# A power on GpSimd between neighbouring indirect transfers, and a new fixed order of all engines' steps

## What is computed

```python
x = _layernorm(x + attn0(x))   # causal, 16 heads of 8, no bias
x = _layernorm(x + ffn0(x))    # top 2 of 8 experts
x = _layernorm(x + attn1(x))   # full, 16 heads of 8, biases
x = _layernorm(x + ffn1(x))    # top 3 of 15 experts, and a shared one

# ffn0, hidden 256
gates, expert_idx = jax.lax.top_k(softmax(xf @ gate_w + gate_b), 2)
h = relu(einsum('nc,ech->neh', xf, w1) + b1)
expert_out = einsum('neh,ehc->nec', h, w2) + b2
out = einsum('ne,nec->nc', weights, expert_out)

# ffn1, hidden 128, the shared expert 256
topk_w, topk_idx = jax.lax.top_k(softmax(xt @ gate_w.T), 3)
topk_w = topk_w / (sum(topk_w) + 1e-20)
h = einsum('td,efd->etf', xt, fc1_w) + fc1_b
a = gelu(h[..., F:]) * h[..., :F] * geglu_mult
yexp = einsum('etf,edf->etd', a, fc2_w) + fc2_b
y = einsum('etd,te->td', yexp, comb) + shared(xt)
```

## Time and profile before

| | |
|---|---|
| median of 3 runs | 944.91 us (943.97 to 946.92) |
| the profiled execution, its span | 1048.6 us |
| instructions | 23098 |
| TensorE busy | 808.7 us, 77% |
| VectorE busy | 657.8 us, 63% |
| ScalarE busy | 500.0 us, 48% |
| GpSimd busy | 429.6 us, 41% |

### The profile page before, as it was taken

How to read it: one execution, slowest core, us unless ns; L and a number is a source line. 1 busy time by engine, 2 the same in 40 slices (tenths; PEclk the granted TensorE clock), 3 DMA queues, 4 the chain that set the end, 5 groups by cost and what they waited for, 6 DMA issues and landing times.

```text
span 1048.6 us, 23098 instructions
## 1 busy us (share of the span) xinstructions
PE 808.7 (77%) x7666; PEld 537.5 (51%) x7666; DVE 657.8 (63%) x1916; ACT 500.0 (48%) x971; POOL 429.6 (41%) x654
## 2 busy tenths in 40 slices
PE   4789878779896878779888797777877795877750
PEld 3456555546664655446545453443444684756640
DVE  2867757666543776767478676786744442565674
ACT  2255545555463565636766465674544252223310
POOL 3002332322144455642354544635366304555565
PEclk9678989989998899888989987987757898899885
DMA  5875866776647551673655543323030387766533
GB/s 122 182 203 149 180 166 178 174 206 157 160 124 147 115 122 44 137 207 109 154 132 122 134 110 75 93 52 72 23 105 33 119 258 242 208 180 188 160 88 83
DMA packets 118772, 144.51 MB, mean 138 GB/s; under 512 B 13155, under 2 KB 92673, under 8 KB 118657
## 3 DMA queue, kind: packets, MB, share of 16 engines
q1 hardware_dynamic: 106689, 121.27, 45.9%
q0 software_dynamic: 10240, 20.99, 7.2%
q10 hardware_dynamic: 1728, 0.79, 0.3%
HBM read 89.78 MB, written 54.41 MB: 138 GB/s over the span
## 4 chain that ended last, share of the span: by engine, by line
PE 26%; DVE 13%; issue 11%; another core or an unknown queue 8%; ACT 4%; DMA 4%; POOL 3%; ACTq 1%; SPq 0%; POOLq 0%; DVEq 0%
DVE mp L1383 4%; PE bank_O L1207 3%; PE bank_FH L1289 3%; PE bank_N L1301 3%; PE pair_T L1188 3%; DMA G<-yd,ypos 2%; ACT P L1021 2%; PE pair_S L1166 2%; PE pair_T L1301 2%; POOL xs L945 1%; DVE X L1588 1%; POOL G L959 1%; PE bank_O L1289 1%; PE bank_M L1127 1%
## 5 line engine op out<-in xcount | busy, mean ns | idle before, releaser
L1383 DVE TENSOR_REDUCE mp<-pair_S 128x4 f32<-128x1024 f32 (+1 forms) x248 | 270.7, 1092 | 149.4 <-PE pair_S L1166 106.0
L1021 ACT ACTIVATE P<-pair_T 128x768 f32<-128x768 f32 (+1 forms) x256 | 234.6, 916 | 122.7 <-PE pair_T L1188 82.6
L959 POOL DMA_INDIRECT G<-yd,ypos x160 | 154.7, 967 | 144.5 <-DMA yd<-yb 57.2
L945 POOL DMA_INDIRECT xs<-X,ypos x160 | 159.6, 997 | 91.9 <-DVE ypos L1535 44.4
L1207 PE MATMUL bank_O<-P,V 128*18 128x256 f32 (+1 forms) x2048 | 131.4, 402 | 2.8 <-issue 2.3
L1188 PE MATMUL pair_T<-QK 51*128 51x256 bf16 (+1 forms) x1024 | 105.9, 282 | 35.3 <-ACT P L1021 27.3
L1166 PE MATMUL pair_S<-QK 48*128 48x256 bf16 (+1 forms) x992 | 101.4, 282 | 20.8 <-DVE mp L1383 12.4
L904 POOL TENSOR_TENSOR rstd<-mv,half 128x2 f32<-128x2 f32 x48 | 9.7, 201 | 213.6 <-DVE mv L1432 211.9
L1207 PEld LDWEIGHTS bank_O<-P,V 128*18 128x18 f32 x2048 | 59.2, 107 | 55.9 <-issue 31.4
L1188 PEld LDWEIGHTS pair_T<-QK 51*128 51x128 bf16 x1024 | 49.1, 100 | 66.7 <-ACT P L1021 38.3
L1150 PE MATMUL pair_T<-bmat 64*128 64x128 bf16 (+1 forms) x544 | 50.9, 265 | 25.2 <-ACT P L1021 20.2
(11 more groups left out here) (172 smaller groups left out, 1437.2 us busy)
## 6 DMA issues: line engine op xcount, KB each, us to landing
QK<-wtab SPq DMA_DIRECT2D x62, 257.0 KB
W<-w_in SPq DMA_DIRECT2D x46, 321.0 KB
yd<-yb SPq DMA_DIRECT2D x53, 256.0 KB
stk<-parts SPq DMA_DIRECT2D x32, 384.0 KB
QK<-stk SPq DMA_DIRECT2D x64, 192.0 KB
xs<-zeros SPq DMA_DIRECT2D x19, 512.0 KB, 5.7
xp<-xs SPq DMA_DIRECT2D x33, 256.0 KB
QK<-stk SPq DMA_DIRECT2D x64, 128.0 KB
```

What stands on the lines that cost most here:

```text
L945: pool.indirect_dma_start(xs[g % 2][0:reach(a) * PAGE], bass.IndirectOffsetOnAxis(ypos[L][:, 2 * b + blk, k:k + 1], 0), X[:, 2 * b + blk, ...
L959: pool.indirect_dma_start(G[i][:, blk, k, :], None, yd[g][0:reach(q) * PAGE], bass.IndirectOffsetOnAxis(ypos[L][:, 2 * b + blk, k:k + 1], 0))\
L1021: act.activation(P[:, i:i + 2, 0:n], pair["T"][:, :].rearrange("p (h c) -> p h c", h=2)[:, :, 0:n], ACT.Exp, scale=SCALE)\
L1383: dve.tensor_reduce(mp[:, a % 2, 0:n, :, 0, p].rearrange("p a r -> p r a"), S, AX.X, ALU.max, negate=True)\
```

## The change

Two things are changed. The list `PLAN` is no longer made by `lay_out`'s play through, but by sorting the steps by a fixed table `BEGINS`, one number for each step. And behind every scatter, and every gather of layer 0, that is followed on POOL directly by another scatter or layer-0 gather, POOL runs a pause: a power of 128x2 values from `half` into the tile `idle`, which nobody reads. That makes 142 pauses, 106 behind scatters and 36 behind layer-0 gathers. A pause waits by a semaphore for the pause before it. No other instruction waits for a pause. The gathers of layer 1 have none. The steps themselves and what they wait for are the same.

```diff
+BEGINS = {
+    "load_xT": (0, 42, 1327, 1896, 2903, 6929, 8462, 10050, 11599, 13183, 14789, 16392, 17960, 19492, 21142, 26465,),
...
 def lay_out(steps):
...
-    while len(order) < len(steps):
-        best = None
...
-        order.append((at, key))
...
-    return [(key[0], key[1:]) for _, key in order]
+    begins = {}
+    for name, times in BEGINS.items():
+        begins.update(zip(sorted(key for key in steps if key[0] == name), times))
+    order = sorted(steps, key=begins.get)
...
+    return [(key[0], key[1:]) for key in order]
...
+POOL_STEPS = ("residual_bias", "inverse_std", "route_diff", "route_pos_mul", "scatter", "gather")
+ON_POOL = [(name, x) for name, x in PLAN if name in POOL_STEPS]
+PAUSES = [step for step, after in zip(ON_POOL, ON_POOL[1:])
+          if all(name == "scatter" or name == "gather" and x[0] < NB for name, x in (step, after))]
...
+        idle = sb("idle", [D, 2])
...
+            def pause(step):
+                if step in PAUSES:
+                    i = PAUSES.index(step)
+                    if i:
+                        pool.wait_ge(paused.sem, i)
+                    pool.tensor_tensor(idle[:, :], half[:, 1, :], half[:, 0, :], ALU.pow).then_inc(paused.sem, 1)
...
+                pause(("scatter", (a, blk, k)))
...
+                pause(("gather", (q, blk, k)))
```

More of the change, by code:

```diff
@@ L411, in plan @@
     return lay_out(steps)
-ENGINES = ("PE", "DVE", "ACT", "POOL", "SP")
-TILING = {"scores": 1, "scores_T": 1, "weigh_V": 2}
-SWITCH = 0.1
-def lay_out(steps):
[L421 to L441, removed]
-    while len(order) < len(steps):
-        best = None
[L444 to L459, removed]
-        order.append((at, key))
[L461 to L474, removed]
-    return [(key[0], key[1:]) for _, key in order]
@@ L478 @@
+def lay_out(steps):
+    begins = {}
+    for name, times in BEGINS.items():
+        begins.update(zip(sorted(key for key in steps if key[0] == name), times))
+    order = sorted(steps, key=begins.get)
+    place = {key: i for i, key in enumerate(order)}
+    assert all(place[k] < place[key] for key, step in steps.items() for k in step[4] if k in place)
+    return [(key[0], key[1:]) for key in order]
 PLAN = plan()
+POOL_STEPS = ("residual_bias", "inverse_std", "route_diff", "route_pos_mul", "scatter", "gather")
@@ L704, in build @@
         out_stored = signal("out_stored")
+        paused = signal("paused")
         def last_norm(k, q):
```

121 lines of the change are left out of this document (added), and 111 rows, old and new, of the table BEGINS.

## The result

The changed kernel takes 997.06 us (median of 4 runs, 986.85 to 998.29) where the kernel before takes 945.91 us (943.97 to 947.50) on the same chip. The ratio is 1.050, 95% interval 1.044 to 1.056: slower by 51 us. The prediction was 937.0 us and a range up to 960.

The account below looks back on a forecast made before the run. No single engine was taken as full; POOL matters only where its transfers stand on the chain. +7.9 + 3.05 − 4.9 − 15 = −8.9 us on 1048.6, scaled to 944.91, gave 937.0 us, range 916 to 960.

Parts of the forecast that it names:

- the new order: All 3897 steps: most stay near their place, only three places differ in a priced way, −4.9 and −15 us.
- The pauses on the chain: 13 neighbouring transfers before 819 us, +7.9 us, and five pauses in batch 31's scatters, +3.05 us; sum +11.0.
- all other pauses I cost at nothing: Pauses off the chain on POOL: covered by POOL's wait for DVE; without that cover up to 76 us.
- The price of a pause: Between two transfers on POOL: starts 1.88 us apart instead of 1.26, costing 0.61 us more; upper bound 1.13 us.
- the slower rival: Pauses on the chain cost 1.13 us each and later combines give nothing: +13 us, about 957 us; chance 0.29.
- The loads of x: Batch 8's xT load is issued up to 6.8 us earlier, shortening TensorE's wait near 135 us: −4.9 us.
- Layer 1's page stretch: Shared_fc rows and norm powers move behind pages or gathers, and TensorE waits less for hT: −15 us.
- 140 or less: Sign in the after profile: this many us from layer 1's first gather to the last end means the page case holds.
- the page case: Rival: layer 1's page stretch gives most of its 38 us, −27 us in all, about 920 us; chance 0.10.
- no gain from pauses: Spacing transfers removes no disturbance, as DVE's combine beside them mostly runs at its minimum; the sum stays +11.0 us.
- Powers that slow VectorE: Rival: pauses stretch DVE instructions beside them, +7.7 us on the chain, about 944 us in all; chance 0.04.
- The clock: Rival: TensorE's granted clock shifts with the order, 0.02 of 0.90 being 18 us either way; chance 0.04.

Follow-up runs that it names:

- e14: The changed kernel without its pauses (new order alone), on a chip where the kernel before takes 944.33 us: 980.37 us, ratio 1.037.
- e2: The changed kernel without its pauses (new order alone), on a chip where the kernel before takes 1064.45 us: 1097.69 us, ratio 1.025.
- e6: The changed kernel without its pauses (new order alone), on a chip where the kernel before takes 1064.53 us: 1103.69 us, ratio 1.039.
- e9: The changed kernel without its pauses (new order alone), on a chip where the kernel before takes 1058.12 us: 1088.30 us, ratio 1.033.
- e18: The changed kernel, unaltered, on another chip where the kernel before takes 947.79 us: 986.44 us, ratio 1.040.
- e5: The changed kernel, unaltered, on a chip where the kernel before takes 1064.53 us: 1040.26 us, ratio 0.978.
- e13: The kernel before, unaltered, profiled again on a chip where its other runs take 944.33 us: 948.69 us, one run.
- e11: The kernel before in its old order with 156 pauses added, on a chip where it takes 949.07 us without them: 1016.23 us, ratio 1.071.
- e17: The changed kernel with one weight build and one xs clearing issued behind batch 9's x load on SP: 991.45 us against 947.79 before, ratio 1.050.

## Why the prediction was wrong, by its steps

**The step that failed** is the one on the new order: "Most of the 3897 steps stand near where they stood. Three places differ in a way that the profile prices." These places were put at −4.9 and −15 us, together −19.9, and all other moves at nothing, without a row that prices them. The order alone measured +36 us (e14, 1.037, interval 1.027 to 1.046), and +30 to +39 us on the slower chips (e2, e6, e9). That is most of the 51 us, and nearly all of the 39 of e18. In e14's trace about half of it is longer matmuls at a lower clock, in layer 1's attention most of all, and about half TensorE standing still, ahead of the 33rd mark in good measure for x, at other loads than the one that was priced. Which moved steps lower the clock stays open.

**The trace** was the wrong one. "That execution ran 11% longer than the median of the runs (944.91), so I carry the share over": the scaling itself moved the sum by 1 us only, from −8.9 to −7.9, but a span 104 us over the times most likely meant another condition of the chip, and it changed what lies on the chain. The earlier trace rows said so: 8% of the chain with an unknown releaser, and I gave these 84 us no thought.

On a chip of the kind that the trace most likely shows, the changed kernel was in fact faster, by 24 us (e5), where the sum said 9. That was luck: the pauses, reckoned at +11, gave −63 there, and the order, reckoned at −19.9, gave +39 (e6). Both terms had the wrong sign.

**The pauses on the chain.** I counted 13 neighbouring pairs and 5 in the last burst from that trace. The same count in e13 gives 53, at my own 0.61 us 32 us in place of 11. For the old order that was the better warning: its pauses cost 67 us. The step "all other pauses I cost at nothing. Their cover is POOL's wait for DVE" failed there: e11 shows that ACT stands for POOL's short steps, which queue behind the bursts. I had read what POOL waits for the earlier trace rows, and not who waits for POOL. In the new order ACT's waits for these steps are small, 6 pauses lie on the chain, and the runs give the pauses 3 to 12 us, not told from nothing. So the +11 us came near the measured size by luck, from a chain that the changed kernel does not have.

**The price of a pause** was mis-sized a little. Two transfers with a power between start 1.98 to 1.99 us apart, not 1.88, as the scatter itself now takes 1.03 us, not 0.96:

```profile
803.98 1.03 POOL L1144 DMA_INDIRECT xs<-X,ypos  x1 [0.20 <-issue]
805.96 1.04 POOL L1144 DMA_INDIRECT xs<-X,ypos  x1 [0.19 <-issue]
807.95 1.03 POOL L1144 DMA_INDIRECT xs<-X,ypos  x1 [0.19 <-issue]
```

So it costs 0.72 us. The gap of 0.19 us was right: it is 0.20 us or less behind 139 of the 142 pauses, so the upper price of 1.13 us, on which the slower rival stood, is not what a pause costs here. Batch 31's burst lasts 9.90 us from first start to last, where 9.4 were given, and 6.4 stood before.

**The loads of x**, −4.9 us: the wait near 135 us is gone, as forecast, but the next load's is 8.5 us, and in sum the sign was wrong. TensorE's waits for x are 17.5 us in six places, longest 8.5, against 12.3 in five in e13. e17 shows that such a wait moves on when its own place is mended.

**Layer 1's page stretch**, −15 us: 3.2 us came (188.2 to 185.1), and they came ahead of the first gather. From the first gather's start to the last one's end it takes 125.5 us, and 123.8 in e13. The sign "140 or less" was met without the page case being true, since before meets it too on this kind of chip. 96 gathers at 1.26 us are 121 us. There was no room left: the 38 us that I took as bound, and the 34.1 us of the earlier trace rows, belong to the other kind of chip. POOL's wait for X is 7.0 us now.

**The rivals.** The slower side was the right one, but not by the pause at the upper price: the order costs TensorE time by itself. In the old order it is a mechanism that I did not list, pauses that delay short steps of the next batch. That the new order gives way to pauses at TensorE's expense fits both, but is not shown. The sentence that reckoned no gain from pauses was wrong for one kind of chip: DVE's combine was the wrong instruction to look at. The combine does run undisturbed; it is the engines that wait for TensorE's results that show it. Powers that slow VectorE did not appear: the combine's mean is 355 ns after and 351 in e13. By the rule of the Trainium skill that I weighed there (GPSIMD Engine Reference, Key points) it might have, and the trace does not show it. The clock did move, as a rival said: 0.905 in e13, 0.884 in e14 and 0.871 after, with TensorE busy for 767, 785 and 790 us. That rival came nearest to a part of the loss, and had a chance of 0.04.

Settled: on chips where before takes 945 us, the result comes from the order (36 us), and the pauses add 3 to 12 us in this order, not told from nothing (67 in the old). On those where it takes 1060, the pauses gain 63 us in the new order and close to nothing in the old. Open: what in a chip makes TensorE's results come late during close transfers, whether it is the pause's length or the power itself that stops this, and which of the moved steps costs the 36 us. No version was found that beats both kernels on both kinds of chip; before is the best on one, the changed kernel on the other.

## What to carry to other kernels

Before a sum is made on a trace, hold its span against the timed runs. If they differ by more than the measurement, find what differs before anything is scaled. A filler on an engine that mostly waits is not free: ask who waits for that engine's short steps behind it, and count the pairs on the chain of a trace that fits the times. Where two changes come together, price and run each alone: here it was the moved steps that cost, not the pauses that had most of the working. A pause that takes away a disturbance is worth as much as the disturbance on that very chip, and it has to be timed on more than one.

## What the runs showed of the hardware that was not expected

The same kernel took 944 to 949 us on two chips and 1058 to 1065 us on three. On the slower ones engines that wait for TensorE stood up to 11.7 us at a time for a releaser that the trace does not know, while indirect transfers of GpSimd started 1.26 us apart, still so at 1.4 us apart, and never at 2.0, with a power between. An indirect transfer behind a power took 1.03 us, against 0.96 behind another transfer.
